# Where the second chunk's queries, keys and values are made: one stretch between the last chunk's routing scores, or spread over the slots behind them

## The reference

```
tok    = ctx @ W_proj + b                      # 1601 x 256
attn   = softmax(x @ tok.T / 16)               # routing scores, 2048 x 1601
routed = attn @ tok
ps_n, in_n = ln(x), ln(routed)
u, r   = sigmoid([ps_n, in_n] @ W_u), sigmoid([ps_n, in_n] @ W_r)
cand   = tanh([r * ps_n, in_n] @ W_n)
x1     = ln((1 - u) * x + u * cand)            # layer 0 ends
h      = ln(x1)
q, k, v = h @ wq.T, h @ wk.T, h @ wv.T         # what the change moves, for 512 of the 2048 tokens
x1     = x1 + attention(q, k, v) @ wo.T        # then cross-attention and MLP
```

## Time and profile before

| | |
|---|---|
| Median of 3 runs | 1515.4 us (1514.67 to 1518.74) |
| The profiled execution | 1512.68 us, its span 1511.0 us |
| Mean granted clock of TensorE | 0.968 of full speed |
| TensorE busy | 1409.6 us, 93% |
| ScalarE busy | 1094.8 us, 72% |
| VectorE busy | 567.5 us, 38% |

### The profile page before, as it was taken

One profiled execution on the slowest core, in us unless ns is written; L12 is line 12 of the kernel. 1 busy time (PEld: TensorE's weight loads), 2 busy tenths in 40 slices (PEclk: granted clock), 3 DMA queues, 4 the chain that ended last, 5 costly groups with the idle time before them and its releaser, 6 DMA issues.

```text
span 1511.0 us, 20524 instructions
## 1 busy us (share of the span) xinstructions
PE 1409.6 (93%) x7934; PEld 623.1 (41%) x7934; DVE 567.5 (38%) x1343; ACT 1094.8 (72%) x1346; POOL 48.7 (3%) x63
## 2 busy tenths in 40 slices
PE   7989899996679999999999998998999999999988
PEld 5668676775422223223222322322323432432347
DVE  5557575777540113303322231440431233143132
ACT  2543444453359999998999998888877787788842
POOL 2000000010010000000000000000000000000000
PEclk9999999998789999999999999999899999999998
DMA  9410001001269000100100353501000000000000
GB/s 298 164 37 1 1 1 56 1 29 51 88 125 148 22 13 12 39 14 15 34 28 12 44 119 48 122 29 47 12 12 15 22 12 12 22 15 1 4 11 14
DMA packets 35048, 66.05 MB, mean 44 GB/s; under 512 B 6203, under 2 KB 20093, under 8 KB 34205
## 3 DMA queue, kind: packets, MB, share of 16 engines
q1 hardware_dynamic: 29580, 43.24, 13.3%
q0 software_dynamic: 5360, 21.37, 3.9%
HBM read 42.70 MB, written 22.02 MB: 43 GB/s over the span
## 4 chain that ended last, share of the span: by engine, by line
PE 67%; ACT 21%; DVE 6%; issue 3%; DMA 2%; SPq 0%; DVEq 0%; POOL 0%; ACTq 0%; POOLq 0%
PE PS L1325 20%; ACT PX L886 19%; PE PS L1308 14%; PE PS L1376 4%; PE PS L1386 3%; PE PS L1361 2%; PE PS L1113 2%; PE PS L1125 2%; PE PS L1116 2%; PE PS L1042 2%; PE PS L1081 1%; PE PS L1082 1%; PE PS L1083 1%; PE PS L1344 1%; PE PS L1459 1%
## 5 line engine op out<-in xcount | busy, mean ns | idle before, releaser
L886 ACT ACTIVATE PX<-PS 128x1024 f32<-128x1024 f32 (+1 forms) x928 | 882.6, 1039 | 136.0 <-PE PS L1308 87.9
L1325 PE MATMUL PS<-PX,V 128*32 128x512 f32 (+1 forms) x3712 | 500.7, 612 | 5.0 <-ACT PX L886 3.0
L1308 PE MATMUL PS<-QST,stack 50*128 50x512 f32 (+1 forms) x1856 | 386.0, 474 | 19.6 <-issue 13.7
L1308 PEld LDWEIGHTS PS<-QST,stack 50*128 50x128 f32 (+1 forms) x1856 | 157.0, 185 | 417.5 <-ACT PX L886 335.5
L1882 DVE COPY OT<-PS 128x512 f32<-128x512 f32 x32 | 22.1, 691 | 310.5 <-PE PS L1325 309.3
L1325 PEld LDWEIGHTS PS<-PX,V 128*32 128x32 f32 (+1 forms) x3712 | 73.9, 108 | 151.3 <-issue 129.3
L755 ACT ACTIVATE PH<-PS 128x512 fp32r<-128x512 f32 (+1 forms) x52 | 31.2, 600 | 79.4 <-PE PS L1062 69.3
L1386 PE MATMUL PS<-W,HIDT 128*128 128x256 f32 x192 | 51.5, 414 | 9.8 <-ACT HIDT L872 9.8
L1376 PE MATMUL PS<-HC,W 128*128 128x512 f32 x96 | 53.2, 641 | 0.0
L1909 DVE RECIPROCAL REC<-REC 128x256 f32<-128x256 f32 x30 | 52.6, 1753 | 1.0
L771 ACT ACTIVATE TR<-PS,small 128x128 f32<-128x128 f32 x32 | 10.0, 363 | 56.7 <-PE PS L1116 56.7
(11 more groups left out here) (194 smaller groups left out, 1461.6 us busy)
## 6 DMA issues: line engine op xcount, KB each, us to landing
QST<-q_parts SPq DMA_DIRECT2D x192, 64.0 KB
q_parts<-PARTS POOLq DMA_DIRECT2D x16, 512.0 KB, 3.6
stack<-k_parts SPq DMA_DIRECT2D x24, 200.1 KB, 6.7
stack<-k_parts SPq DMA_DIRECT2D x18, 256.0 KB
k_parts<-KPARTS POOLq DMA_DIRECT2D x8, 512.0 KB, 3.2
v_cross<-V POOLq DMA_DIRECT2D x1, 3328.0 KB, 12.3
V<-v_cross SPq DMA_DIRECT2D x2, 1664.0 KB, 13.7
k_parts<-PARTS POOLq DMA_DIRECT2D x6, 512.0 KB, 3.4
```

The source lines that it names most:

```text
L886: act.activation(PX[0:kr, (2 * t + half) % 4, :, :], PS[0:kr, slot:slot + 2, :], ACT.Exp, scale=SCALE).then_inc(at["exp"], 1)
L1308: ins = pe.matmul(PS[0:kr, 2 * (n % LOOK) + jj, :], KST[a][lo:lo + NROW, pair, kt * P:kt * P + kr].bitcast(F32R), QST[lo:lo + NROW, pair, ...
L1325: ins = pe.matmul(PS[32 * j:32 * j + 32, 6, :], V[0:kr, kt, 2 * (g // 2 * GH + j) + g % 2, :], PX[0:kr, (2 * t + j // 2) % 4, j % 2, :], s ...
```

## The change

The ten entries of chunk 1 are no longer placed in slots 16 and 17. They are done in one stretch at the end of slot 14, between the routing scores of steps 48 and 49 (of 52). Their banks change from (0, 1, 4, 5) to (0, 1, 2, 3), since banks 4 and 5 hold the routing product there: entries 10 to 19 use banks 2, 3, 0, 1, 2, 3, 0, 1, 2, 3. Nothing is added or removed; chunks 0, 2 and 3 stay where they are.

```
-    DENSE = {10: 0, 22: 3}
-    FIRST, SECOND = stage3[1], stage3[2]
-    EARLY = {16: FIRST[0:4], 17: FIRST[8:10], 21: SECOND[8:10]}
-    LATE = {16: FIRST[4:8], 19: SECOND[0:4], 20: SECOND[4:8]}
+    DENSE = {10: 0, 14: 1, 22: 3}
+    SECOND = stage3[2]
+    EARLY = {21: SECOND[8:10]}
+    LATE = {19: SECOND[0:4], 20: SECOND[4:8]}
...
     def qkv_bank(u):
-        return (0, 1, 2, 3)[u % 4] if u < 10 else (0, 1, 4, 5)[u % 4]
+        return (0, 1, 2, 3)[u % 4] if u < 20 else (0, 1, 4, 5)[u % 4]
```

## The result

The changed kernel is slower. Over 20 runs each, its median is 1523.28 us (1518.06 to 1526.44) against 1514.98 us (1509.39 to 1519.15): a ratio of 1.005, 95% interval 1.0038 to 1.0062, which is +7.6 us (+5.8 to +9.4); the medians themselves are 8.3 us apart. The forecast was +5.5 us and 1520.9 us: the measured 1523.28 lies within the stated range of 1516.0 to 1524.5, and +5.5 just under the interval. In a later session, with 12 and 23 runs, the same kernel gave 1.0029 (1.0013 to 1.0046), +4.4 us. The two intervals overlap, and the forecast lies between the two values. The profiled execution had a span of 1519.6 us against 1511.0 us.

What follows compares the result with a forecast made beforehand. TensorE was taken to bound up to slot 15, and from slot 18 a ring through VectorE, TensorE and ScalarE. Adding 14.3 us and giving back 8.8 makes +5.5 us, 1520.9 us at the median; range 1516.0 to 1524.5.

Steps and rivals of the forecast that it cites:

- The wait ahead of the stretch: End of slot 14: the first moved matmul waits for hF of tile 7, adding 1.77 us.
- The stretch: Between scores 48 and 49: the ten entries, priced from chunk 0's like stretch behind slot 10, take 12.5 us.
- Added in all: Slot 14: wait for hF plus the ten entries, 1.77 + 12.5 = 14.3 us, bounds 11.3 and 14.7.
- The drain's give-back: Slots 16 and 17, emptied of the entries: 2.9 + 5.9 = 8.8 us come back, of 16.0 us of TensorE's list.
- the ring: Drain slots: dependency loop VectorE norms, TensorE hats and candidate, ScalarE tanh, VectorE; one turn 12.70 us, 11.1 at full clock.
- rival of a drain bound by TensorE: Slots 16 and 17: TensorE's list sets them, all 16.0 us come back; -1.7 us, 1513.7 us; chance 0.11.
- the faster one: Slots 14 to 17: all 16.0 us come back and the stretch costs only 11.3; -4.7 us, 1510.7; chance 0.05.
- From slot 18 on: Slot 18 to the first attention scores: instruction lists do not differ, so no gain or loss was put there.
- a clock that stays up: Slot 17: candidate runs at full rate, giving back 1.6 us more; +3.9 us, 1519.3 us; chance 0.20.
- the one turn I charged to it: Slot 17: TensorE idles about 3 us, candidate then runs at 1.2 GHz; turn 12.70 us, 1.6 more than at full clock.
- rival of a clock that falls further: Slots 17 and 18: gates at 1.2 GHz too, about 1 us more in each; +7.5 us, 1522.9 us; chance 0.12.
- a sign of being wrong: Profile after: turns longer than 12.7 us in emptied slots 16 and 17, meaning something else binds them.

Runs made afterwards that it cites:

- the stretch behind slot 15: The changed kernel with the ten entries placed behind slot 15 instead of slot 14: 1522.06 us, ratio 1.0032 against the kernel before.
- the run with matmuls alone: The kernel before with 13 matmuls that nobody reads added behind slot 14, no entry moved: 1528.32 us, ratio 1.0077 against the kernel before.
- the second profile: The changed kernel profiled once more with no further change; tile 7's transpose to first attention score took 137.01 us, ratio 1.0029 in that session.
- all gaps filled: Unread matmuls in TensorE's waits: kernel before (slots 18, 19, 21, 22) 1511.36 us, ratio 0.9964; changed kernel (also slot 17) 1515.22 us, ratio 0.9995.
- two gaps filled: The changed kernel with 3 unread matmuls between gates and hats in slots 17 and 18: 1522.18 us, ratio 1.0026 against the kernel before.

## Why the prediction was right

**The wait ahead of the stretch**: forecast 1.77 us, measured 308.75 - 306.83 - 0.14 = 1.78. Its cause was half told: besides hF of tile 7 it is bank 2, as the stretch behind slot 15 showed.

**The stretch**: forecast 12.5 us, measured 12.57, with the same waits as chunk 0's and with the shorter one at score 49's bank (0.54 instead of 0.86). **Slot 15** cost what it did. **Added in all**: forecast 14.3, measured 14.35; the run with matmuls alone confirms that this work is on the path one for one.

**The drain's give-back**: slots 16 and 17 were to give 2.9 and 5.9 us; they gave 1.9 and 6.2 in one profile and 2.8 and 5.6 in the other, 8.1 and 8.3 in all for 8.8. That the ring limits it, and not the 16.0 us of TensorE's work, held. This refutes the rival of a drain bound by TensorE, and with it the faster one, whose stretch would also have had to pack. Slot 16's turn was the forecast one where its gates ran at the full clock (11.25 us for 11.1).

**From slot 18 on** I had put nothing, since the lists do not differ. It was 0.7 us (78.22 us from norms of slot 18 to the first attention score, before 77.49) and 0.9 in the second profile. With all gaps filled the same distance is 72.60 us in the changed kernel and 72.99 in the one before, so this was the clock. The two terms missed in the same direction, this one put 0.7 us too low and the give-back 0.5 to 0.7 too high: 7.0 us for 5.5 in the stage. Whether the +7.6 us of the first session holds more than the stage's 7.0, or the +4.4 us of the second less, the intervals do not settle.

**The clock.** The profile shows 0.50 in slot 17's candidate, behind the gap of 3.25 us; that decided for the forecast and against the case of a clock that stays up. The rule of the Trainium skill ("TensorE: Matmul & The Clock Gate", section "HAM oscillation — how this bites in real kernels"), that waits between short bursts of matmuls lower the clock of the next burst, agrees with it. The clock also cost more than the one turn I charged to it: of the 7.0 us some 3 to 3.5 are clock by the pair of filled kernels, against 1.6 in my sum.

**The rival of a clock that falls further** came nearest in its number (+7.5 us, 1522.9), but not by what it told: it put the 2 us into slow gates of slots 17 and 18, and these ran at the full rate in both profiles (1.95 and 1.89 us). Slow gates came in slot 16, in one profile of two, and cost 0.9 us; the rest came behind slot 18. I had named turns over 12.7 us in the emptied slots as a sign of being wrong. Slot 17 took 13.00 us in the second profile: its hats and both halves of its candidate ran at the lower clock (1.11, 2.07 and 1.91 us), so this too was the clock.

## What to carry to other kernels

Work that fills another engine's waits is cheap where it is; moved to a place where its engine is the bound, it costs all its matmuls and the waits for its inputs and its buffers besides, and gives back no more than the difference between the old turn of the ring and the turn of the empty ring. Price both ends from stretches of the trace that already look like the new ones. Compare stages only down to the parts that differ, and in more than one execution: here the last stretch's first matmuls differed by 1.5 us between two executions of one kernel, and the last wait by 1.8 us between kernels with the same lists there. Where an entry waits for the reader of its own bank, moving it on by one slot can be worth more than another place for the whole: here two entries moved by one slot made the kernel 0.2% faster (ratio 0.9978, 0.9962 to 0.9993), and all ten moved together made it slower.

## What the runs showed that was not expected

Matmuls that nobody reads, put where TensorE waits anyway, made both kernels' stages shorter: with all gaps filled by 6.8 us in the changed kernel (137.08 to 130.30) and by 3.3 in the one before. With two gaps filled the two turns fell to 11.2 us, but the whole stage did not show it (137.11 us).

Where a dip falls differs from execution to execution. In the kernel before with fillers even a slot without any change of its own, slot 17, took 19.83 instead of 18.6 us, its candidate being slow from first to last (1.91 us for each half); and the same first matmuls of the last stretch took 5.08 or 6.54 us in two executions of the changed kernel.

Short stretches are dear: four entries with 5.2 us of matmuls held up the next scores by 9.0 us, ten entries with 11.3 us by 14.4 (by what the waits add, 3.8 and 3.1 us).
